# Feed-forward of a language-model layer: product kept in PSUM, outputs between the shared halves, row statistics at the group border

## What is computed

```python
h = h + ffn(layernorm(h))            # h: 8192 tokens x 512

def ffn(x2):
    shared = (x2 @ sw1.T * sqrelu(x2 @ swg.T)) @ sw2.T      # hidden 256
    xl = x2 @ Wdown.T                                       # latent 128
    probas = sigmoid(x2 @ Wg.T)                             # 16 experts
    # the 8 best of probas + biases, normalised, times 2.5 -> w_dense (0 for the others)
    for e in range(16):
        ye = (xl @ rw1[e].T * sqrelu(xl @ rwg[e].T)) @ rw2[e].T   # hidden 256
        acc = acc + w_dense[:, e:e+1] * ye
    return shared + acc @ Wup.T      # sqrelu(z) = relu(z) ** 2
```

## Time and profile before

| | |
|---|---|
| median of 3 runs | 2818.55 us (2815.9 to 2821.38) |
| profiled execution | 2816.09 us, its span 2814.3 us |
| PE busy | 2586.7 us (92%) |
| DVE busy | 1937.4 us (69%) |
| ACT busy | 1816.8 us (65%) |
| POOL busy | 1199.5 us (43%) |
| L1494 DVE, weighing | 605.5 us in 512, mean 1.183 |
| L1127 POOL, low part of a unit | 738.2 us in 512, mean 1.452 |
| L1487 DVE, product | 372.3 us in 544, mean 0.684 |

### The profile page before, as it was taken

How to read it: one execution, slowest core, us unless ns; L and a number is a source line. 1 busy time by engine, 2 the same in 40 slices (tenths; PEclk the granted TensorE clock), 3 DMA queues, 4 the chain that set the end, 5 groups by cost and what they waited for, 6 DMA issues and landing times.

```text
span 2814.3 us, 48768 instructions
## 1 busy us (share of the span) xinstructions
PE 2586.7 (92%) x13025; PEld 1862.8 (66%) x13120; DVE 1937.4 (69%) x3742; ACT 1816.8 (65%) x4597; POOL 1199.5 (43%) x1275
## 2 busy tenths in 40 slices
PE   3899999999999999679999999999999999999998
PEld 2566656666666666457777777777777777777776
DVE  4666666666666665486786686687677668668667
ACT  2666666666666667376675675676566567567566
POOL 3333333333333333044454464454445445446445
PEclk8999999999999999799999999999999999999999
DMA  3111111222211111343132122212213212221222
GB/s 104 24 61 60 60 60 60 65 66 64 64 60 60 60 45 59 103 120 99 38 98 83 53 82 83 80 48 90 80 40 94 83 46 89 83 68 63 87 67 58
DMA packets 99807, 197.67 MB, mean 70 GB/s; under 512 B 10928, under 2 KB 10928, under 8 KB 99568
## 3 DMA queue, kind: packets, MB, share of 16 engines
q1 hardware_dynamic: 94576, 179.29, 19.4%
q0 software_dynamic: 5120, 17.31, 2.8%
HBM read 128.89 MB, written 34.08 MB: 58 GB/s over the span
## 4 chain that ended last, share of the span: by engine, by line
issue 28%; POOL 26%; DVE 2%; PE 1%; ACT 1%; POOLq 1%; DMA 0%; SPq 0%; DVEq 0%; ACTq 0%
POOL t_lo L1127 24%; POOL sh_lo L1127 1%; DVE t L1494 1%; DVE t L1487 1%; POOLq L1125 0%; DVE f_lo L1512 0%; DMA x<-h 0%; ACT x L1286 0%; PE fwork L1142 0%; PE fwork L1143 0%; PE fwork L1144 0%; DMA w_rows<-wT 0%; PE fwork L1166 0%; DVE fxT_lo L1433 0%; PE ps_u L1142 0%
## 5 line engine op out<-in xcount | busy, mean ns | idle before, releaser
L1127 POOL TENSOR_TENSOR t_lo<-t,t_hi 128x512 fp32r<-128x512 f32 x512 | 738.2, 1452 | 469.8 <-ACT t_hi L1341 469.5
L1494 DVE TENSOR_TENSOR t<-t,w_all 128x512 f32<-128x512 f32 x512 | 605.5, 1183 | 35.7 <-DMA w_all<-w_rows 7.7
L377 POOL TENSOR_TENSOR probs<-probs,inv 128x512 f32<-128x512 f32 x256 | 265.0, 1041 | 626.8 <-DVE inv L774 626.6
L1487 DVE TENSOR_TENSOR t<-ps_u,square 128x512 f32<-128x512 f32 x544 | 372.3, 684 | 207.0 <-PE ps_u L1144 125.5
L599 ACT ACTIVATE probs<-ps_s,nmax 128x128 f32<-128x128 f32 x1024 | 362.5, 370 | 222.6 <-DVE nmax L769 222.6
L1341 ACT ACTIVATE t_hi<-t 128x512 fp32r<-128x512 f32 x512 | 320.6, 626 | 249.4 <-DVE t L1494 246.9
L1324 ACT ACTIVATE square<-ps_g 128x512 f32<-128x512 f32 x544 | 316.3, 581 | 91.3 <-PE ps_g L1144 89.3
L1328 ACT ACTIVATE square<-square 128x512 f32<-128x512 f32 x544 | 344.0, 632 | 17.3
L488 PE MATMUL ps_s<-k_diag,qT 128*128 128x512 f32 x512 | 263.9, 597 | 7.8 <-DVE qT L745 1.1
L1142 PE MATMUL ps_y<-t_hi,f_hi 128*128 128x512 f32 x512 | 227.3, 444 | 40.2 <-POOL t_lo L1127 39.3
L769 DVE TENSOR_REDUCE nmax<-ps_s 128x4 f32<-128x512 f32 x256 | 176.1, 688 | 102.2 <-PE ps_s L488 100.7
(11 more groups left out here) (195 smaller groups left out, 5449.4 us busy)
## 6 DMA issues: line engine op xcount, KB each, us to landing
w_all<-w_rows SPq DMA_DIRECT2D x256, 256.0 KB, 3.2
res_next<-h SPq DMA_DIRECT2D x64, 256.0 KB, 2.3
res<-res_next SPq DMA_DIRECT2D x64, 256.0 KB, 2.3
h<-res SPq DMA_DIRECT2D x64, 256.0 KB, 2.0
x<-h SPq DMA_DIRECT2D x16, 1024.0 KB, 6.0
fres<-h SPq DMA_DIRECT2D x16, 1024.0 KB, 7.6
out<-fres SPq DMA_DIRECT2D x64, 256.0 KB, 2.2
fres<-in_w_ffn SPq DMA_DIRECT2D x14, 512.0 KB, 3.7
```

The source lines that it names most:

```text
L377: pool.tensor_tensor(probs[:, s % 4, :, :], probs[:, s % 4, :, :], inv[:, s % 4, :].rearrange("p (h o) -> p h o", o=1).to_broadcast([P, HP ...
L1127: pool.tensor_tensor(lo, t[:, t_slot(j), :], hi.bitcast(F32), ALU.subtract).then_inc(t_lo_done, 1)
L1487: dve.tensor_tensor(t[:, t_slot(j), :], ps_u[:, j % 2, :], square[:, j % 2, :], ALU.mult).then_inc(t1_done, 1)
L1494: dve.tensor_tensor(t[:, t_slot(j), :], t[:, t_slot(j), :], w_all[:, e % 2, :], ALU.mult).then_inc(t_done, 1)
```

## The change

`linear` of a hidden unit writes its product back into the unit's own `ps_u` bank, and `weigh` reads it there and writes `t`. The shared halves still go to `t`. `ps_u` gets a third bank, and `first_products` waits for `weigh` three units back (`u_left`). In the border PE does: logits turn, shared half 0, weights turn, four outputs, shared half 1. The rows of group g+2 (no longer g+1 within the loop) get statistics and normalisation at the border between g and g+1, on DVE between the output additions, on ACT ahead of shared half 1; SP loads them at the end of the group, ahead of the store of `w_rows`. The transposes move to units 8, 14, 20 and 26. Before group 0, the rows of group 1 are prepared too. Group 14 is written out as well.

```diff
-F_STATS, F_MOMENTS, F_SEED, F_RSTD, F_SHIFT, F_XN, F_XT = (
-    (3, 5, 7, 9), 10, 11, (12, 13, 14), 15, (17, 18, 19, 20), (20, 23, 26, 29))
+U_BANKS = 3
+F_XT = (8, 14, 20, 26)
...
-        ps_u = pb("ps_u", [P, 2, TOK], F32)
+        ps_u = pb("ps_u", [P, U_BANKS, TOK], F32)
...
+        def u_bank(j):
+            return 1 - j if j < HC else (j - HC + 1) % U_BANKS
+        def u_left(engine, g, j):
+            n = j - HC
+            if n < 0:
+                at_least(engine, t_done, UNITS * (g - 1) + UNITS - 2 - j + 1)
+            elif n == 0:
+                engine.wait_ge(t1_done, ALL_UNITS * g + 1)
+            elif n == 1:
+                at_least(engine, t_done, UNITS * g)
+            elif n == 2:
+                engine.wait_ge(t1_done, ALL_UNITS * g + 2)
+            else:
+                engine.wait_ge(t_done, UNITS * g + n - U_BANKS + 1)
...
             spread(0, 1)
+            load_x(1, 0)
             def group(g, more):
-                if more:
-                    load_x(g + 1, g)
...
+                if has_next(g, 2):
+                    load_x(g + 2, g + 1)
                 if more:
                     store_rows(g + 1)
...
             def first_products(g, n):
...
+                pe.wait_ge(relu_done, ALL_UNITS * g + HC + n - 1)
+                split_matmul(ps_g[:, (HC + n) % 2, :], wts(F_EXP + e * E_COLS + HID + j * P, P),
+                             xl, True, True).then_inc(g_full, 1)
+                u_left(pe, g, HC + n)
+                split_matmul(ps_u[:, u_bank(HC + n), :], wts(F_EXP + e * E_COLS + j * P, P),
+                             xl, True, True).then_inc(u_full, 1)
...
                     shared(g + 1, 0)
-                    shared(g + 1, 1)
                     weights_turn(g + 1, half)
                 for i in range(TILES):
                     output(g, out_half(g), i)
+                if more:
+                    shared(g + 1, 1)
...
                     squares_end(g, HC + n)
-                    hidden_hi(g, HC + n - 1)
+                    if n > 0:
+                        hidden_hi(g, HC + n - 1)
-                    if more and n in F_XN:
-                        normalise(g + 1, F_XN.index(n))
...
                     squares(g + 1, 0)
+                    weights_copy(g + 1, half)
                     squares_end(g + 1, 0)
+                    hidden_hi(g + 1, 0)
+                    if has_next(g, 2):
+                        for i in range(TILES):
+                            normalise(g + 2, i)
                     squares(g + 1, 1)
                     squares_end(g + 1, 1)
-                    weights_copy(g + 1, half)
-                    hidden_hi(g + 1, 0)
+                    hidden_hi(g + 1, 1)
...
             hidden_hi(0, 0)
+            hidden_hi(0, 1)
+            for i in range(TILES):
+                normalise(1, i)
             group(0, True)
...
+                product = ps_u[:, u_bank(j), :]
+                if j < HC:
+                    at_least(dve, t_lo_done, t_slot_left(g, j))
+                    dst = t[:, t_slot(j), :]
+                else:
+                    dst = product
+                dve.tensor_tensor(dst, product, square[:, j % 2, :], ALU.mult).then_inc(t1_done, 1)
             def weigh(g, j):
...
-                dve.tensor_tensor(t[:, t_slot(j), :], t[:, t_slot(j), :], w_all[:, e % 2, :],
+                at_least(dve, t_lo_done, t_slot_left(g, j))
+                dve.tensor_tensor(t[:, t_slot(j), :], ps_u[:, u_bank(j), :], w_all[:, e % 2, :],
                                   ALU.mult).then_inc(t_done, 1)
...
                 sum_lo(g)
+                ahead = has_next(g, 2)
                 if more:
                     routing(g + 1, half)
-                    linear(g + 1, 0)
-                    linear(g + 1, 1)
+                if ahead:
+                    for i in range(TILES):
+                        x_moments_of(g + 2, i)
                 for i in range(TILES):
                     add_out(g, i)
+                    if more and i == 0:
+                        linear(g + 1, 0)
+                    if ahead and i == 1:
+                        x_moments_of(g + 2, TILES)
+                        x_seed(g + 2)
+                    if ahead and i == 2:
+                        x_rstd(g + 2, 0)
+                        x_rstd(g + 2, 1)
+                if ahead:
+                    x_rstd(g + 2, 2)
+                    x_shift(g + 2)
+                if more:
+                    linear(g + 1, 1)
...
             split(7)
+            for part in range(TILES + 1):
+                x_moments_of(1, part)
+            x_seed(1)
+            for k in range(3):
+                x_rstd(1, k)
+            x_shift(1)
             group(0, True)
```

More of the change, by code:

```diff
@@ L1028, in drained, with has_next @@
             engine.wait_ge(work_free[k % 2], half + k // 2 + 1)
+        def has_next(g, ahead):
+            return not isinstance(g, int) or g + ahead < GROUPS
         def front_half(g):
@@ L1111, in _ @@
             group(0, True)
-            with sp.Fori(1, GROUPS - 1) as g:
+            with sp.Fori(1, GROUPS - 2) as g:
                 group(g, True)
+            group(GROUPS - 2, True)
             group(GROUPS - 1, False)
@@ L1195, in shared @@
                 n = ALL_UNITS * g + j
[L1196 to L1202, removed]
+                at_least(pe, relu_done, n - 1)
+                for m in range(DC):
+                    mm = split_matmul(ps_g[:, j % 2, :], wts(F_SG + m * HID + j * P, P), xs(m),
+                                      m == 0, m == DC - 1)
+                mm.then_inc(g_full, 1)
+                u_left(pe, g, j)
+                for m in range(DC):
+                    mm = split_matmul(ps_u[:, u_bank(j), :], wts(F_S1 + m * HID + j * P, P), xs(m),
+                                      m == 0, m == DC - 1)
+                mm.then_inc(u_full, 1)
             def first_products(g, n):
                 e, j = divmod(n, HC)
[L1207 to L1212, removed]
+                xl = xl_hi[:, :], xl_lo[:, :]
+                pe.wait_ge(relu_done, ALL_UNITS * g + HC + n - 1)
[4 more added lines that the diff above has]
+                             xl, True, True).then_inc(u_full, 1)
             def second_product(g, n):
@@ L1277, in _ @@
             group(0, True)
-            with pe.Fori(1, GROUPS - 1) as g:
+            with pe.Fori(1, GROUPS - 2) as g:
                 group(g, True)
+            group(GROUPS - 2, True)
             group(GROUPS - 1, False)
@@ L1399, in _ @@
             hidden_hi(0, 0)
+            hidden_hi(0, 1)
+            for i in range(TILES):
+                normalise(1, i)
             group(0, True)
-            with act.Fori(1, GROUPS - 1) as g:
+            with act.Fori(1, GROUPS - 2) as g:
                 group(g, True)
+            group(GROUPS - 2, True)
             group(GROUPS - 1, False)
@@ L1485, in linear @@
                 dve.wait_ge(u_full, n + 1)
-                at_least(dve, t_lo_done, t_slot_left(g, j))
-                dve.tensor_tensor(t[:, t_slot(j), :], ps_u[:, j % 2, :], square[:, j % 2, :],
-                                  ALU.mult).then_inc(t1_done, 1)
+                product = ps_u[:, u_bank(j), :]
[5 more added lines that the diff above has]
+                dve.tensor_tensor(dst, product, square[:, j % 2, :], ALU.mult).then_inc(t1_done, 1)
             def weigh(g, j):
@@ L1522, in group @@
                     if more:
-                        if n in F_STATS:
-                            x_moments_of(g + 1, F_STATS.index(n))
-                        if n == F_MOMENTS:
-                            x_moments_of(g + 1, TILES)
-                        if n == F_SEED:
-                            x_seed(g + 1)
-                        if n in F_RSTD:
-                            x_rstd(g + 1, F_RSTD.index(n))
-                        if n == F_SHIFT:
-                            x_shift(g + 1)
                         if n in F_XT:
@@ L1571, in _ @@
             split(7)
+            for part in range(TILES + 1):
[4 more added lines that the diff above has]
+            x_shift(1)
             group(0, True)
-            with dve.Fori(1, GROUPS - 1) as g:
+            with dve.Fori(1, GROUPS - 2) as g:
                 group(g, True)
+            group(GROUPS - 2, True)
             group(GROUPS - 1, False)
```

## The result

The changed kernel takes 2745.97 us (median of four runs, 2745.62 to 2747.06); the kernel before, on the same chip, 2818.09 (2815.9 to 2821.38). The ratio is 0.9744, 95% interval 0.9727 to 0.9761. The forecast was 2728 in a range of 2704 to 2772: right in sign and range; it put the gain 18 us too high.

The account below looks back on a forecast made before the run. PE was taken as the bound, with 8.8 us of gaps in each 101.06 us turn. Fourteen turns win 90.5, the last group 5.1, the start loses 5.9: 89.7 off 2816.09 gives 2726.4, set at 2728, range 2704 to 2772.

Parts of the forecast that it names:

- The floor of 92.3 us a turn: One feed-forward turn of 416 matmuls if PE never waited; of today's 101.06 us, 8.8 are gaps in PE.
- Product in PSUM: Unit loop: two unblocked DVE passes take 1.33 us a unit against PE's 2.06, so PE becomes the bound.
- the slower rival: Unit loop: the in-place PSUM product takes 1.83 us at the far end, 251 us more, 2979; chance 0.05.
- The shared port: Unit loop: the weighing could still wait for POOL; 42 us less won, 2770; chance 0.08.
- Third bank: Unit loop: the ps_u bank is already free some 3 us early, so a third one wins nothing.
- Statistics and normalisation at the border: Between groups: preparation leaves the loop; gaps 2.3 us a turn instead of 8.8, new turn 94.6, 90.5 us won.
- third step and shift end at 1915.3: Border, on DVE: when the last Newton step and shift finish; ACT then normalises until 1918.4, unit 0's Relu at 1920.9.
- The loop gaps go: Unit loop: chain latency about 5.4 us against 6.9 given by Y_LAG, so PE's waits there vanish.
- SP's queue: Row load for group g+2 ahead of the w_rows store lands some 9 us before the statistics, at no cost.
- Prologue and group 0: Preparing group 1's rows before group 0 loses 15.4 us; group 0 itself wins 9.5; together 5.9 lost.
- Last group: Group 15: start 1.2, 28 units 2.4, and a drain 1.5 shorter; 5.1 us won.
- the late border: Border: ACT later than scheduled, paid every turn; 2 us x 15 = 30 less won, 2758; chance 0.12.

Follow-up runs that it names:

- the best version: Kernel with old border order, normalisation in the unit loop and earlier row load; ACT's rounding of shared half 1 put behind unit 0's squares: 2694.75 us, ratio 0.9565.
- the product alone: Kernel before, with only the product kept in PSUM and three ps_u banks; border order, statistics and normalisation as before: 2716.76 us, ratio 0.9644.
- the moves alone: Whole change, but the product goes through the SBUF tile t as before: 2797.58 us, ratio 0.9926.
- the early load: Whole change, with the rows of group 1 loaded ahead of the ninth weight piece: 2738.22 us, ratio 0.9713.
- normalisation in the loop: Whole change, but ACT normalises the next rows in units 5, 11, 17 and 23 instead of at the border and ahead of group 0: 2718.98 us, ratio 0.9643.

## Why the prediction was right, and where it was off

**What bounds the kernel.** Right. The floor of 92.3 us a turn stands: in the turn of the table above, whatever PE's starts are apart beyond the spacings of the earlier trace rows adds up to 3.7, and 96.0 less 3.7 is 92.3. In the best version 93.70 with a wait of 0.5 agrees with it.

**Product in PSUM.** Right in mechanism, durations and effect. The form that no row showed, the pass in place, took 0.70 us at most, 8 ns above the 0.69 assumed; the slower rival, which needed 1.5, is false. The shared port is false too: the pass that reads PSUM and `w_all` was never stretched in 512. The Trainium skill, "SBUF — State Buffer", section on who interferes with whom, has it that a DVE instruction outside the 2-port modes contends with GpSimd only if it has two SBUF inputs; the weighing agrees (694 ns at most, 1825 when its product goes back to SBUF). By the fixed costs in the Trainium skill, "VectorE: DVE Perf Modes", errata section, 120 cycles from PSUM against 58 from SBUF, the PSUM source should by estimate cost 0.065 us more; the runs show none in the weighing (medians of 692 from PSUM, 691 unblocked from SBUF).

**Third bank.** Right: nothing.

**Statistics and normalisation at the border.** This term was mis-sized. It said "2.3 us a turn instead of 8.8"; it was 3.7. Term by term: the gap before `ps_g` of unit 2 was to be 0.5 and was 1.1 (0.94 of wait, the rest restart); the gap before the first `ps_y` was to be 1.2 and was 1.4; the small remainder was to be 0.6 and was 1.2. The step that failed is "third step and shift end at 1915.3". All its instructions were priced at their unblocked duration, although the same schedule puts the linear product of shared half 0 just ahead of them, and ACT's and POOL's passes for that half follow it. The conflict that the change removes from the weighing was left out here. It went through ACT (the last engine at the border, as said) to PE: Relu of unit 0 was 0.6 late against the forecast, and so was the gap before `ps_g`. Moving one ACT instruction took the step's 1.06 us away and, with it, 15.2 us in the turns. That this is near the 18 missed is partly chance, for it also removed the 0.5 of wait that the forecast had counted. The other 0.8 of the 1.4 us are the small restarts, 1.2 instead of 0.6, and 0.2 more before `ps_y`; some 0.3 of these come with the loop, since the turn that leads out of it is 0.3 shorter.

**What the forecast did not ask** is what this part is worth once the first is in. It added both into one new turn. The two single-part kernels show 101.06 going to 94.85 by the product alone, to 99.1 by the moves alone, and to 96.02 by both. The words "The loop gaps go" already held the answer: with the loop's gaps gone, there is next to nothing to win by emptying the loop. What is left is the price at the border, with 2.9 us of ACT and the stretched step in one chain (a turn of 96.02 instead of 94.85), and 16.1 us once, ahead of group 0.

**SP's queue.** Right for the loop: no wait on a row load there. At the start the load stayed "behind the weight rows, as today", and that place is 10.0 of the 14.3 us, as the early load showed. The forecast had the price, but took the place as given.

**Prologue and group 0.** -15.4 and 9.5, measured -15.4 and 9.95 by the same starts. First weighing expected at 1222.0, seen at 1221.99; PE idled 21.22 us before `ps_g` of unit 0, expected 21. The exact hit is luck: the attention phase ended 1.1 later in the execution after, and from there on the loss was 14.3.

**Last group.** 5.1 expected, 3.25 by the weighing's start. 1.5 of the difference is a stretch at half clock in the tail, which the kernel before had not (last section).

**Rivals and chances.** The sign is beyond doubt by the runs. The time lies between the forecast and the late border, 18 above 2728 and 12 below 2758. The late border is the rival that came true in part: 1.4 us a turn instead of 2, of which one stretched instruction made about 0.6, where the forecast named ACT's four passes and the number of the steps.

## What to carry to other kernels

Ask of each part of a change what it is worth after the others are in: work moved off an engine wins only as long as that engine is late, and at its new place it costs whatever chain it stands in. Before pricing a row of small dependent steps at their usual duration, look whether another engine's pass stretches them at that moment, as POOL's did here; moving one operand of the weighing to PSUM freed both sides. A load that many wait for is worth a look at its place in the queue before anything is computed faster.

## What the runs showed of the hardware

**A tiny instruction waits for a whole POOL pass.** A DVE instruction of 128x4 with two SBUF inputs took 1.22 us instead of 0.16 beside a POOL pass of 1.29, fourteen times, and 0.164 at most where the pass came later.

**A product in place in PSUM costs nothing to speak of**: 700 ns against 691 into SBUF.

**A late start that comes with the loop.** The weighing, which reads that product, starts 0.2 to 0.3 us late 104 times (21.8 us of DVE's idle time in all, in the line L1537 of the page above), as in the 0.26 here, on DVE's timeline:

```profile
2185.68 0.69 DVE L1537 TENSOR_TENSOR t<-ps_u,w_all 128x512 f32<-128x512 f32 x1 [0.26 <-DVE ps_u L1530]
```

That unit is the one for which PE waits at the group's start. The 104 are eight units, always the same, in each of groups 1 to 13. In groups 0, 14 and 15, which are written out, there is none, though the product is in place there too, so it is not the in-place product alone. With the product in SBUF (the moves alone) the trace lists no such idle time either. The change also puts one more semaphore wait in front of the weighing (`t_slot_left`); whether that is the cause was not tested.

**A half clock in the tail.** In the changed kernel PE's matmuls in the last outputs slow down for a while. PE's timeline, and the stretch in the table (granted clock after the busy times):

```profile
2730.78 0.47 PE L1167 MATMUL fwork<-f_hi,sh_hi 128*128 128x512 f32 x1 [1.50 <-DVE t_lo L1542]
...
2731.56 0.58 PE L1167 MATMUL fwork<-f_hi,sh_hi 128*128 128x512 f32 x1
...
2735.20 0.39 PE L1167 MATMUL fwork<-f_hi,sh_hi 128*128 128x512 f32 x1
```

```profile
2731.60:2735.00 3.40, 3.40 (x10) 2.66 (x9) 0.69 (x1) 0.00 (x0) 0.00 (x0) 0.50 0.00 0
```

Nine matmuls from 2731.56 to 2735.20 take 3.64 us instead of 2.10 at the spacing of the earlier trace rows, with a granted clock of 0.50 (1.2 GHz). It came in five of the profiled executions (the whole change, the moves alone, normalisation in the loop, the early load, unit 0 ahead) and not in the other five, nor in the kernel before, with the same 1.50 us of PE's idle time just ahead. Why in these is open.

**The attention phase ends at another time from one profiled execution to the next**, by up to 5.7 us, with the same code. Differences of that size between two kernels that change only the phase behind it are better read from the start of that phase.
